# Relations 0 to 3 of a graph layer: seven half-size block products each in place of a full product, in two passes over the left operands, with sums of weight quarters on GpSimd

## The chip, the core and the metric

The kernel runs on one core of one Trainium2 chip. Its engines are TensorE (PE), VectorE (DVE), ScalarE (ACT), GpSimd (POOL) and SyncE (SP, which here only issues transfers). Each engine works through its own instructions strictly in the order in which the program lists them and waits for another engine or a transfer by a semaphore. The metric is the device time of one execution in microseconds (us).

## The reference, cut to what matters

The network takes x (1250 nodes, 1024 features) and 40000 edges (src, dst, type 0 to 7). The part that changes is the relational graph convolution:

```python
xn = _layernorm(x, axis=-1)
def _rgcn(x, edge_index, edge_type, weight, root, bias):
    out = x @ root + bias
    for r in range(8):
        mask = (edge_type == r)
        sums = segment_sum(x[src] * mask[:, None], dst)
        cnt = segment_sum(mask, dst)
        out = out + (sums / maximum(cnt, 1)[:, None]) @ weight[r]
    return out
```

A linear attention, two gates and an LSTM-like step follow, all with 1024x1024 weights and the same 1250 rows; the change doesn't touch them.

## The kernel before

**Products.** The kernel computes y_r = xn @ weight[r] for all eight relations first and gathers rows of y per edge afterwards. The work of TensorE is a list of stages. A stage is one half (512 columns) of one product; it has 10 units, one for each tile of 128 nodes. A unit is 24 matmuls of 512 columns into one PSUM bank: 8 blocks of the inner dimension, three matmuls each, since both operands are split into a high and a low part (`aThi`, `aTlo` for the left, `Whi`, `Wlo` for the weights). q numbers the units through the whole kernel, k the 8 blocks in a unit. The other engines' programs are written as a loop over the same (q, k), so that a step's place (q, k) sets its place in the order of its engine.

**Weights.** A stage's weights come in four granules of 128x1024 (512 KB). SP loads one into `Wraw`, ACT rounds it (`hi_w`, Whi), DVE subtracts (`lo_w`, Wlo). `Wraw` lies in the same bytes as `Wlo`. There are two sets, used by stages in turn, so the granules of stage s+1 are loaded, rounded and subtracted while stage s is computed.

**Results.** ACT copies a finished unit of y to one of three places of `res` (`evict`) and SP stores it to y_d (`store_unit`).

**Edges.** While relations 0 to 3 are computed, DVE also orders the edges: `count_below`, `run_codes`, `run_half`, `hold_half`, then for 2 halves x 10 tiles a `top_of` (five MAX8 with four MATCH_REPLACE8 between) and a `rank_tile`, and for each half `tables` and `tables_weights`. POOL reads 20 runs of codes (`read_run`, after `run_places` on DVE) and sends 10 rows of tables per half (`send_rows`, after `tables_weights`); SP then reads them back (`load_edges`, which waits for `sent[h]`). From q = 82 on POOL gathers rows of y (`gather`) and DVE adds them up (`add_edges`).

**The start.** x comes in ten tiles: LN on DVE (`ln_x`), TensorE turns the tile, ACT and DVE split it. POOL forms x + xn (`rows_sum`): tile 0, then the codes of the edges, then tiles 1 to 9. SP's `x_rows(t)` waits for `rows_sum(t)` and stores.

Of the kernel before, what the change touches and what calls it, by code (L numbers as in the profile page):

```python
# [5 lines left out]
F32 = mybir.dt.float32  # L6
# [74 lines left out]
Y_, R_, V_, K_, X_, G_, Q_, O_, C_, I_, T_, F_ = range(12)  # L81
STAGE = [(Y_, r, h) for r in range(R) for h in range(2)]
# [5 lines left out]
BY_ACT = (Y_, V_)  # L88
# [37 lines left out]
LN_AT = {1: 2, 2: 3, 4: 4, 6: 5, 7: 6, 8: 7, 9: 8, 10: 9}  # L126
TURN_AT = {1: 1, 3: 2, 5: 3, 7: 4, 8: 5, 9: 6, 10: 7, 11: 8, 12: 9}
# [90 lines left out]
def build(nc, x, src, dst, edge_type, weight, root, bias, w_gate, b_gate, Wq, Wk, Wv, Wg, bg, Wo,  # L218
          W_iT, b_i, W_oT, b_o, W_cT, b_c, out):
    with ExitStack() as ctx:  # L220
# [9 lines left out]
        xs_d = dram("xs_d", [N, D])  # L230
        y_d = [dram(f"y_d{h}", [HALF_R * N, D]) for h in range(2)]
# [110 lines left out]

        x_raw = at(M + 16448, "x_raw", [128, D], F32R)
# [27 lines left out]
        acc = ctx.enter_context(nc.psum_tensor("acc", [128, 3, H], F32))  # L371
        agg = ctx.enter_context(nc.psum_tensor("agg", [128, 2, H], F32))
# [3 lines left out]
        def turned_rows(w):  # L376
# [37 lines left out]
        v_in = [sem(f"v_in{i}") for i in range(2)]  # L414
        neg, expd, kv_zero, kv_done, kv_sb = (
            sem(n) for n in ("neg", "expd", "kv_zero", "kv_done", "kv_sb"))
        g_in = [sem(f"g_in{i}") for i in range(6)]
        num_done, num_out, gated, o_turned, o_hi, o_lo = (
            sem(n) for n in ("num_done", "num_out", "gated", "o_turned", "o_hi", "o_lo"))
        xs_in = [sem(f"xs_in{i}") for i in range(2)]  # L420
        tx_in = [sem(f"tx_in{i}") for i in range(2)]
        th_st = [sem(f"th_st{i}") for i in range(TH_SEMS)]
        u_in = [sem(f"u_in{i}") for i in range(U_SEMS)]
        th_tanh, th_made, u_turned, u_hi, u_lo = (
            sem(n) for n in ("th_tanh", "th_made", "u_turned", "u_hi", "u_lo"))
        c_in = [sem(f"c_in{i}") for i in range(3)]
        p_made, x1_made, x1_st, ln2_var, ln2_root, ln2_ready, ln2_done, x1_turned, x1_hi, x1_lo = (
            sem(n) for n in ("p_made", "x1_made", "x1_st", "ln2_var", "ln2_root", "ln2_ready", "ln2_done",
                             "x1_turned", "x1_hi", "x1_lo"))
        gate_act, cell, cell_th, out_made = (sem(n) for n in ("gate_act", "cell", "cell_th", "out_made"))  # L430
# [17 lines left out]
        def load_beside(q):  # L448

            if q < 20:  # L450
                return range(2 * GRAN, 3 * GRAN) if q == LAST[0] + 1 else range(0)
            s, i = UNIT[q]
            n = GRAN * (s + 1) + i
            return range(n, n + 1) if s + 1 < STAGES and i < GRAN else range(0)

        def split_beside(q):

            if q < 20:
                return {17: range(8, 9), 18: range(9, 11), 19: range(11, 12)}.get(q, range(0))
# [26 lines left out]
        def wait_evicted(engine, q):  # L486

            if KIND[q] in BY_ACT:
                engine.wait_ge(evac_a, BY_ACT_TO[q])
            else:  # L490
                engine.wait_ge(evac_v, BY_DVE_TO[q])

# [59 lines left out]
        def f_count(n):  # L552

            return 48 * len(range(n % 3, 2 * T, 3)) + 16 * (n // 3 + 1)
# [8 lines left out]
        def _(sp):  # L563
            def load_w(n):
                s, g = divmod(n, GRAN)
                if s >= 2:
                    sp.wait_ge(prod, LAST[s - 2] + 1)
                sp.dma_start(granule(Wraw, n), source_of(s)[g * 256:(g + 1) * 256, :].rearrange("(b p) n -> p b n", p=128)
                             ).then_inc(w_raw[n % (2 * GRAN)], 16)

            def load_x(t):
                sp.dma_start(xr[0:width(t), t % XS, :], x[rows(t), :]).then_inc(x_in[t % XS], 16)
# [11 lines left out]
            def load_bias(n):  # L584
                s = BIASED[n]
                if n >= 2:
                    wait_evicted(sp, LAST[BIASED[n - 2]])
# [102 lines left out]
            def load_o(t):  # L690
                g = min(t // 3, 2)
                if t == 3 * g:
                    sp.wait_ge(rows_st, 16 * (8 if g == 2 else 2 * g + 2))
                if t >= 2:
                    sp.wait_ge(o_in[t % 2], quarters_in(t - 2, 2))
# [97 lines left out]
            for n in range(4):  # L793
                load_w(n)
            load_x(1)
            load_w(4)
            load_w(5)
            load_x(2)
            load_w(6)
            load_w(7)  # L800
# [8 lines left out]
            def x_rows(t):  # L809

                sp.wait_ge(ln_done, with_halves(t))
                sp.dma_start(xn_d[rows(t), :], xnb[0:width(t), t % XS, :]).then_inc(xn_st[t % XS], 16)
                sp.wait_ge(xs_made, t + 1)
                sp.dma_start(xs_d[rows(t), :], xr[0:width(t), t % XS, :]).then_inc(xs_st[t % XS], 16)
# [7 lines left out]
            for q in range(UNITS + 1):  # L822
# [4 lines left out]
                if q < UNITS:  # L827
                    s, i = UNIT[q]
                    kind, _, h = STAGE[s]
# [1147 lines left out]
```

## Time and profile before

| | |
|---|---|
| median of three runs | 2173.67 us (2172.82 to 2173.79) |
| profiled execution, first to last instruction (span) | 2172.2 us |
| TensorE busy | 2156.8 us (99%) |
| VectorE busy | 1224.3 us (56%) |
| ScalarE busy | 441.0 us (20%) |
| GpSimd busy | 717.5 us (33%) |
| moved by DMA | 437.58 MB, mean 201 GB/s |

The span is the time from the first to the last instruction of one profiled execution; a run's device time is 1.5 us above it at the median. Busy time is an average over stages with different limits, so what a change of one stretch is worth has to be read in that stretch. A busy TensorE means that a matmul is in flight; the matmuls overlap.

### The profile page before, as it was taken

The numbers are of one execution on the slowest core, as the hardware profiler recorded it, in microseconds if no ns is written. First come the engines' busy times: TensorE is split into PE (matmuls) and PEld (weight loads), VectorE is DVE, ScalarE is ACT, GpSimd is POOL, SyncE is SP. The second block draws the span as 40 slices with busy tenths as digits, with TensorE's granted clock in tenths as the row PEclk, the third lists the DMA queues.
The fourth block names the chain that finished last, engine by engine and source line by source line (L and its number), as shares of the span: only waits on it lengthen the run. The fifth ranks groups of instructions, "written<-read, shape, count | busy, mean of one in ns | idle before, by whom it ended". The sixth has DMA issues, their size and how long they took to land.

```text
span 2172.2 us, 25195 instructions
## 1 busy us (share of the span) xinstructions
PE 2156.8 (99%) x9802; PEld 1744.3 (80%) x9802; DVE 1224.3 (56%) x1648; ACT 441.0 (20%) x618; POOL 717.5 (33%) x631
## 2 busy tenths in 40 slices
PE   8999999999999999999999999999999999999999
PEld 6877888888888888888878778889988888788877
DVE  6332678736666666676666567663355658534233
ACT  3221111211111111100221211112232313321121
POOL 4103002055555556553646445541221353000000
PEclk9999999999999999999999999999999999999999
DMA  6543321447688988793978888864169988604102
GB/s 255 191 133 94 111 87 48 132 165 240 233 296 288 306 307 287 248 307 94 339 238 291 282 272 297 304 206 159 68 184 265 295 288 260 176 16 132 56 28 80
DMA packets 217649, 437.58 MB, mean 201 GB/s; under 512 B 37381, under 2 KB 69812, under 8 KB 217530
## 3 DMA queue, kind: packets, MB, share of 16 engines
q1 hardware_dynamic: 146458, 239.60, 33.6%
q0 software_dynamic: 65248, 191.13, 26.7%
q10 hardware_dynamic: 5824, 5.25, 1.0%
q8 instruction: 77, 1.26, 0.2%
q14 instruction: 42, 0.34, 0.1%
HBM read 363.07 MB, written 113.90 MB: 220 GB/s over the span
## 4 chain that ended last, share of the span: by engine, by line
PE 98%; DVE 1%; ACT 0%; DMA 0%; issue 0%; SPq 0%; DVEq 0%; ACTq 0%
PE acc L1018 91%; PE acc L1013 5%; PE agg L951 1%; PE misc L936 1%; PE tp L900 0%; DVE Wlo L1211 0%; DMA x1n_d<-lnb 0%; DMA xr<-in_x 0%; PE agg L1026 0%; PE acc L1026 0%; DVE stats L1259 0%; DVE aTlo L1221 0%; ACT aThi L1045 0%; PE tp L908 0%; DVE res L1623 0%
## 5 line engine op out<-in xcount | busy, mean ns | idle before, releaser
L1018 PE MATMUL acc<-Whi,aThi 128*128 128x512 f32 (+1 forms) x2872 | 1136.2, 396 | 2.8 <-DVE A L1573 1.1
L1018 PE MATMUL acc<-Whi,aTlo 128*128 128x512 f32 (+1 forms) x2872 | 1131.9, 394 | 0.0
L1018 PE MATMUL acc<-Wlo,aThi 128*128 128x512 f32 (+1 forms) x2872 | 1128.5, 393 | 0.0
L1018 PEld LDWEIGHTS acc<-Whi,aThi 128*128 128x128 f32 (+1 forms) x2872 | 532.7, 185 | 134.5 <-DVE A L1573 1.5
L1018 PEld LDWEIGHTS acc<-Whi,aTlo 128*128 128x128 f32 (+1 forms) x2872 | 532.7, 185 | 133.5
L1018 PEld LDWEIGHTS acc<-Wlo,aThi 128*128 128x128 f32 (+1 forms) x2872 | 533.8, 186 | 131.9
L1818 POOL DMA_INDIRECT ring<-y_d,edge x390 | 482.4, 1237 | 430.0 <-DVE U L1443 156.9
L1211 DVE TENSOR_TENSOR Wlo<-Wraw,Whi 128x1024 fp32r<-128x1024 f32 x152 | 185.7, 1225 | 321.6 <-ACT Whi L1037 282.6
L1053 ACT COPY res<-acc 128x512 f32<-128x512 f32 (+1 forms) x180 | 105.7, 587 | 833.0 <-PE acc L1018 747.6
L1443 DVE SCALAR_TENSOR_TENSOR U<-ring,edge,U 128x1024 f32<-128x1024 f32 x180 | 230.3, 1279 | 16.6 <-DMA ring<-y_d,edge 16.3
L1443 DVE SCALAR_TENSOR_TENSOR odd<-ring,edge,odd 128x1024 f32<-128x1024 f32 x170 | 217.5, 1280 | 22.6 <-DMA ring<-y_d,edge 22.5
L1037 ACT CAST Whi<-Wraw 128x1024 fp32r<-128x1024 f32 x152 | 158.8, 1047 | 152.2 <-DMA Wraw<-in_L_mix_Wg 49.1
L1573 DVE TENSOR_TENSOR res<-acc,bias_sb 128x512 f32<-128x512 f32 x99 | 68.5, 692 | 214.0 <-PE acc L1018 126.7
L1805 POOL DMA_INDIRECT slot_d<-table,slot x20 | 21.7, 1087 | 227.9 <-DVEq L1403 222.4
L1114 ACT ACTIVATE res<-res 128x512 f32<-128x512 f32 (+1 forms) x59 | 37.4, 633 | 282.9 <-DVE res L1573 282.9
L1552 DVE SCALAR_TENSOR_TENSOR res<-acc,res 128x512 f32<-128x512 f32 (+3 forms) x44 | 28.0, 637 | 99.5 <-ACT res L1066 99.5
L1013 PE MATMUL acc<-aThi,Whi 128*128 128x384 f32 (+1 forms) x192 | 69.5, 362 | 0.0
L1940 POOL TENSOR_TENSOR og<-og,part 128x384 f32<-128x384 f32 (+1 forms) x32 | 27.7, 876 | 122.6 <-DVE part L1603 122.6
L1013 PE MATMUL acc<-aThi,Wlo 128*128 128x384 f32 (+1 forms) x192 | 67.6, 352 | 0.0
L1013 PE MATMUL acc<-aTlo,Whi 128*128 128x384 f32 (+1 forms) x192 | 67.5, 352 | 0.0
L1064 ACT ACTIVATE res<-acc 128x512 f32<-128x512 f32 (+3 forms) x44 | 24.4, 556 | 182.0 <-PE acc L1013 89.0
L1798 POOL DMA_INDIRECT runs<-code_d,run_row x20 | 21.1, 1054 | 100.4 <-DVEq L1299 94.7
(183 smaller groups left out, 1055.9 us busy)
## 6 DMA issues: line engine op xcount, KB each, us to landing
y_d<-res SPq DMA_DIRECT2D x144, 256.0 KB
Wraw<-in_L_gnn_weight SPq DMA_DIRECT2D x64, 512.0 KB
Wraw<-in_L_gnn_w_gate SPq DMA_DIRECT2D x16, 512.0 KB
ring<-y_d,edge POOLq DMA_INDIRECT x390
xr<-in_x SPq DMA_DIRECT2D x9, 512.0 KB, 4.7
xn_d<-xnb SPq DMA_DIRECT2D x9, 512.0 KB, 5.4
xs_d<-xr SPq DMA_DIRECT2D x9, 512.0 KB, 5.9
ur_d<-res SPq DMA_DIRECT2D x18, 256.0 KB
```

Of the source, the lines that this page charges most:

```text
L1013: mm = nc.tensor.matmul(to, a[:, s % 2, k, cols], b[:, k, c0:c0 + w], start=start, stop=stop)
L1018: mm = nc.tensor.matmul(to, a[:, k, rows(i)], b[:, s % 2, k, :], start=start, stop=stop)
L1037: nc.scalar.copy(granule(Whi, n), granule(Wraw, n)).then_inc(w_hi, 1)
L1053: nc.scalar.copy(res[0:width(i), q % 3, :], acc[0:width(i), q % 3, :]).then_inc(evac_a, 1)
L1064: nc.scalar.activation(a, p, ACT.Relu, scale=-1.0).then_inc(neg, 1)
L1114: nc.scalar.activation(a, a, ACT.Tanh if kind == T_ else ACT.Sigmoid).then_inc(gate_act, 1)
L1211: nc.vector.tensor_tensor(granule(Wlo, n), granule(Wraw, n), granule(Whi, n).bitcast(F32), ALU.subtract).then_inc(w_lo, 1)
L1443: nc.vector.scalar_tensor_tensor(to, g, scale, to, ALU.mult, ALU.add).then_inc(u_acc, 1)
L1552: nc.vector.scalar_tensor_tensor(a, p, 0.0, a, ALU.max, ALU.add).then_inc(evac_v, 1)
L1573: nc.vector.tensor_tensor(to, p, bias_sb[0:w, n % 2, :], ALU.add).then_inc(evac_v, 1)
L1818: pool.indirect_dma_start(ring[:, j % RING, :], None, a, bass.IndirectOffsetOnAxis(ap=index, axis=0), bounds_check=top - 1, oob_is_err=Fal ...
L1940: nc.gpsimd.tensor_tensor(o, o, part[0:w, a % 2, n, :], ALU.mult).then_inc(gated, 1)
```

## The change

Each y_r of relations 0 to 3 is now computed by blocks: the nodes are halved (2 x 625), and so are the inner dimension and the columns (512). Seven products of half size replace eight, with sums of quarters of the weights and of the left operand, and earlier results taken in again. Relations 4 to 7 and all later stages are as before.

- A block product has 5 units (m = 0 to 4, tiles of 125 nodes), and a unit now has 12 matmuls. Stages of four kinds come one kind after the other: AL (q 0 to 39), BE (40 to 79), GA (80 to 119), one stage for each relation, two products in each (p = 0 and 1); then DE (120 to 139), one product per relation. Where p = 1 follows in the same bank, it adds to what p = 0 left there, after that was copied out.
- Five banks are used in turn; `BEFORE[q]` is the unit whose copy must be done before unit q may start. In AL, BE and GA the order of units is m0 m1 of p = 0, m0 of p = 1, m2, m1, m3, m2, m4, m3, m4.
- Weights: BE needs eight loads of 512 KB and three sums of 128x1024 for each p on POOL (`add_quarters`), of which the third is stored to t4_d (`store_t4`) and read again for DE; GA needs six loads and one sum per p. BE's granules 2 and 3 are rounded only when the store of the third sum is done, since `Whraw` lies in the same bytes as `Whi`.
- All 140 units leave through a ring of four places (`made`); AL, BE and DE by ACT (`evict_made`), GA by DVE, which adds an earlier result (`evict_added`). The first product of BE and all of DE start from an earlier result that SP loads three units ahead (`load_part`) and ACT writes negated into the bank (`seed`).
- The left operand's four quadrants are combined on DVE (`make_right`), stored, and exchanged between the kinds of stages (six loads of 1.28 MB, `load_left`, split by `hi_left` and `lo_left`).
- The work on the edges is placed anew: `edge_at` puts old place (q, k) at 35 + (q - 17) x 13/8 new units.

```diff
+SEVEN = list(range(HALF_R))
+STAGE = [(AL_, r, 0) for r in SEVEN] + [(BE_, r, 0) for r in SEVEN] + [(GA_, r, 0) for r in SEVEN]
+STAGE += [(DE_, r, 0) for r in SEVEN[::2]]
+IN_TURN = [0, 1, 5, 2, 6, 3, 7, 4, 8, 9]
+UNIT = [(s, 5 * p + m) for m in range(3) for p in range(2) for s in range(2)]
+UNIT += [(s, 5 * p + m) for s in range(2) for p in range(2) for m in (3, 4)]
+UNIT += [(s, i) for s in range(2, STAGES) for i in
+         (range(10) if STAGE[s][0] == DE_ else IN_TURN if STAGE[s][0] in BLOCKED else range(units_of(s)))]
...
+        _at = [FIRST[_s] + d for d in {BE_: (5, 8, 9, 10), GA_: (4, 5, 6, 8)}.get(STAGE[_s + 1][0], (3, 5, 6, 8))]
...
+def edge_at(q, k):
+    return divmod(280 + (8 * (q - 17) + k) * 13 // 8, 8)
...
+            def store_made(q):
+                wait_evicted(sp, q)
+                sp.dma_start(block_rows(q), made[0:SIDE, q % OUT_RING, :]).then_inc(made_st[q % OUT_RING], 16)
...
+                    if q + 3 < BLOCK_UNITS and q + 3 in IN_PLACE:
+                        load_part(q + 3)
-                    if q == 76:
+                    if q == edge_at(76, 0)[0]:
                         load_edges(1)
...
+                if kind in BLOCKED:
+                    if BEFORE[q] is not None:
+                        wait_evicted(pe, BEFORE[q])
+                    if seeded_unit(q):
+                        pe.wait_ge(seeded, SEEDS_TO[q])
...
+                    for k in range(4):
+                        beside(q, k)
+                        if m == 0 and k % 2 == 0:
+                            pe.wait_ge(w_lo, SPLIT_RANK[GRAN * s + 2 * p + k // 2] + 1)
...
+            def evict_made(q):
+                if q >= OUT_RING:
+                    wait_made_stored(act, q - OUT_RING)
+                act.wait_ge(prod, q + 1)
+                nc.scalar.copy(made[0:SIDE, q % OUT_RING, :], acc[0:SIDE, BANK[q], :]).then_inc(evac_a, 1)
...
+            def evict_added(q):
+                n = IN_PLACE[q]
+                wait_made_stored(dve, q - OUT_RING)
+                dve.wait_ge(part_in[n % IN_RING], 16 * (n // IN_RING + 1))
+                dve.wait_ge(prod, q + 1)
+                nc.vector.tensor_tensor(made[0:SIDE, q % OUT_RING, :], acc[0:SIDE, BANK[q], :], in_place(q), ALU.add
+                                        ).then_inc(evac_v, 1)
...
+                add(second, granule(Whraw, n))
+                add(first, second)
+                add(granule(Whraw, n + 2), first)
...
+            for q in range(BLOCK_UNITS):
+                s = UNIT[q][0] + 1
+                if s > 2 and STAGE[s][0] in SUMS_IN:
+                    for p in range(2):
+                        if q == FIRST[s - 1] + 3 + 2 * p:
+                            add_quarters(s, p)
+                if q == edge_at(28, 2)[0]:
...
+                            read_run(i, t)
+                for h in range(2):
+                    if q == edge_at(59 + 15 * h, 1)[0]:
...
+                            send_rows(h, t)
```

Three places show what the new order puts side by side.

On DVE, before, these rows stood in the stage of relation 2 (`Wlo` is `lo_w`, MAX and MATCH_REPLACE are `top_of`, `above` and `rank` are `rank_tile`):

```order
L1211 TENSOR_TENSOR Wlo<-Wraw,Whi 128x1024
L1344 TENSOR_SCALAR above<-keyrow,key 128x1280
L1345 TENSOR_REDUCE rank<-above 128x1
L1355 MAX top_codes<-held 128x8
L1357 MATCH_REPLACE held<-top_codes,held 128x128
```

Now the same steps stand between the copies of GA's units (`made<-acc`); these are DVE's rows at q = 105 to 108:

```order
L1597 TENSOR_TENSOR Wlo<-Wraw,Whi 128x1024
L1640 TENSOR_TENSOR made<-acc,res 125x512
L1597 TENSOR_TENSOR Wlo<-Wraw,Whi 128x1024
L1640 TENSOR_TENSOR made<-acc,res 125x512
L1768 TENSOR_SCALAR above<-keyrow,key 128x1280
L1769 TENSOR_REDUCE rank<-above 128x1
L1640 TENSOR_TENSOR made<-acc,res 125x512
L1779 MAX top_codes<-held 128x8
```

What moved: rows that a bank, and with it TensorE, waits for now stand in this order, with steps of the edges between them.

On POOL, before, nothing stood between the last `rows_sum` and the sending of tables but the reads of runs:

```order
L1781 TENSOR_TENSOR xr<-xr,xnb 128x1024 [waits ln_done] x8
L1781 TENSOR_TENSOR xr<-xr,xnb 98x1024 [waits ln_done]
L1798 DMA runs<-code_d,run_row 128x64 [waits xn_st2,xs_st2,xs_st1,xn_st3,xn_st1,xs_st3,xs_st0,run_made,xn_st0,codes_st]
L1798 DMA runs<-code_d,run_row 128x64 x19
L1805 DMA slot_d<-table,slot 1280x82 [waits tabled,ranked]
```

Now at q = 53 to 55 (BE of relation 1; the sums are for BE of relation 2, which starts at q = 60):

```order
L2227 TENSOR_TENSOR Whraw<-Whraw,Wraw 128x1024 [waits w_sum_p_made]
L2260 DMA runs<-code_d,run_row 128x64 [waits xn_st2,xs_st2,xs_st1,xn_st3,xn_st1,xs_st3,xs_st0,run_made,xn_st0,codes_st]
L2260 DMA runs<-code_d,run_row 128x64 x19
L2227 TENSOR_TENSOR Wraw<-Wraw,Whraw 128x1024 [waits w_raw3,w_add_g_in1]
L2227 TENSOR_TENSOR Wraw<-Wraw 128x1024 [waits w_sum_p_made,w_raw1]
L2227 TENSOR_TENSOR Whraw<-Whraw,Wraw 128x1024 [waits w_sum_p_made]
```

What moved: the 20 reads stand between the sums for p = 0 and those for p = 1.

On SP, before, the second half's table was read at q = 76 in 11 transfers, the first of which waits for `sent[1]`. The last two of them and what stands behind:

```order
L668 DMA edge<-slot_d 128x24
L670 DMA whose<-slot_d 128x10x2
L620 DMA y_d<-res 128x512 [waits evac_a] x4
L620 DMA y_d<-res 98x512 [waits evac_a]
L568 DMA Wraw<-in_L_gnn_weight 128x2x512 [waits prod]
```

Now it is read at q = 130, again with the wait at the first of the 11; the earlier result for unit 133 is loaded ahead of them, that for unit 134 is the fifth row here:

```order
L941 DMA edge<-slot_d 128x24
L943 DMA whose<-slot_d 128x10x2
L840 DMA y_d<-made 125x512 [waits evac_a]
L760 DMA Wraw<-in_L_gnn_weight 128x2x512 [waits prod]
L835 DMA bias_sb<-y_d 125x512 [waits made_st_g_in1,seeded_ln2_root]
L840 DMA y_d<-made 125x512 [waits evac_a]
```

What moved: loads that TensorE needs within four units now queue behind the wait for `sent[1]`.

## Rows read from the trace of the kernel before

**Rows 1.** The page: busy time and share of the span, instructions
```profile
PE 2156.8 (99%) x9802; PEld 1744.3 (80%) x9802; DVE 1224.3 (56%) x1648; ACT 441.0 (20%) x618; POOL 717.5 (33%) x631
```

**Rows 2.** The chain that ended last: start us, us, what
```profile
89.76 372.25 PE acc L1018 x1608
```

**Rows 3.** Timeline of PE at its first matmuls: start us, us, engine
```profile
10.35 0.80 PE L1018 MATMUL acc<-Whi,aThi 128*128 128x512 f32 x1 [0.66 <-DVE aTlo L1668]
...
14.78 0.40 PE L1018 MATMUL acc<-Wlo,aThi 128*128 128x512 f32 x1
15.02 0.39 PE L1018 MATMUL acc<-Whi,aTlo 128*128 128x512 f32 x1
...
17.80 0.39 PE L1018 MATMUL acc<-Whi,aTlo 128*128 128x512 f32 x1
19.17 0.50 PE L1018 MATMUL acc<-Whi,aThi 128*128 128x512 f32 x1 [0.98 <-DVE Wlo L1211]
```

**Rows 4.** Busy time by stretch, with the columns of its heading
```profile
core 0: us, PE busy (x) PEld busy (x) DVE busy (x) ACT busy (x) POOL busy (x), PEclk, DMA share, GB/s
278.00:334.00 56.00, 56.00 (x243) 44.84 (x243) 41.39 (x109) 10.11 (x15) 0.00 (x0) 1.00 0.27 84
334.00:389.00 55.00, 55.00 (x240) 44.01 (x239) 42.11 (x107) 7.10 (x12) 11.23 (x10) 1.00 0.25 68
389.00:445.00 56.00, 56.00 (x244) 44.84 (x243) 43.94 (x98) 12.12 (x18) 5.27 (x5) 1.00 0.35 115
```

**Rows 5.** Timeline of DVE: one rank_tile, one top_of, the next rank_tile
```profile
313.48 0.88 DVE L1344 TENSOR_SCALAR above<-keyrow,key 128x1280 f32<-128x1280 f32 x1
...
315.92 0.29 DVE L1355 MAX8 top_codes<-held 128x8 f32<-128x128 f32 x1
...
319.12 0.89 DVE L1344 TENSOR_SCALAR above<-keyrow,key 128x1280 f32<-128x1280 f32 x1
```

**Rows 6.** Timeline of DVE: tables (to the Wlo) and tables_weights
```profile
341.36 0.17 DVE L1349 CAST slot<-rank 128x10 int32<-128x10 f32 x1
...
345.70 1.22 DVE L1211 TENSOR_TENSOR Wlo<-Wraw,Whi 128x1024 fp32r<-128x1024 f32 x1 [0.17 <-ACT Whi L1037]
...
352.49 2.03 DVE L1383 SCALAR_TENSOR_TENSOR of_r<-relation,weigh 128x400 f32<-128x400 f32 x4
...
361.29 0.89 DVE L1344 TENSOR_SCALAR above<-keyrow,key 128x1280 f32<-128x1280 f32 x1
```

**Rows 7.** Groups by line: busy us, mean ns, idle before and releaser
```profile
L1211 DVE TENSOR_TENSOR Wlo<-Wraw,Whi 128x1024 fp32r<-128x1024 f32 x152 | 185.7, 1225 | 321.6 <-ACT Whi L1037 282.6
L1573 DVE TENSOR_TENSOR res<-acc,bias_sb 128x512 f32<-128x512 f32 x99 | 68.5, 692 | 214.0 <-PE acc L1018 126.7
L1037 ACT CAST Whi<-Wraw 128x1024 fp32r<-128x1024 f32 x152 | 158.8, 1047 | 152.2 <-DMA Wraw<-in_L_mix_Wg 49.1
L1053 ACT COPY res<-acc 128x512 f32<-128x512 f32 (+1 forms) x180 | 105.7, 587 | 833.0 <-PE acc L1018 747.6
```

**Rows 8.** Groups of POOL by line, the same columns
```profile
L1781 POOL TENSOR_TENSOR xr<-xr,xnb 128x1024 f32<-128x1024 f32 (+1 forms) x10 | 23.9, 2401 | 46.2 <-DVE xnb L1274 25.1 <-DVE Wlo L1211 21.1
L1948 POOL TENSOR_TENSOR cring<-cring 128x512 f32<-128x512 f32 (+1 forms) x20 | 29.5, 1476 | 1.6
```

**Rows 9.** Timeline of POOL: the first and the last of the 20 reads of runs
```profile
175.02 1.28 POOL L1798 DMA_INDIRECT runs<-code_d,run_row  x1 [94.66 <-DVEq L1299]
...
200.88 1.00 POOL L1798 DMA_INDIRECT runs<-code_d,run_row  x1 [0.30 <-issue]
```

**Rows 10.** Timeline at 36 to 42 us: SP's queue, and ACT's copy
```profile
36.19 0.32 SPq L814 DMA_DIRECT2D xs_d<-xr  x1
...
37.03 0.78 SPq L620 DMA_DIRECT2D y_d<-res  x1
...
41.84 0.58 ACT L1053 COPY res<-acc 128x512 f32<-128x512 f32 x1 [7.08 <-DMA y_d<-res]
```

**Rows 11.** Timeline at 437 to 458 us: DVE, and SP's queue
```profile
437.27 0.17 DVE L1401 COPY table<-cnt 128x10 f32<-128x10 f32 x1
...
452.82 4.59 SPq L668 DMA_DIRECT2D edge<-slot_d  x10
457.46 0.44 SPq L670 DMA_DIRECT2D whose<-slot_d  x1
```

**Rows 12.** Transfers: issues with KB each, us to landing
```profile
xn_d<-xnb SPq DMA_DIRECT2D x9, 512.0 KB, 5.4
fx<-x_d SPq DMA_DIRECT2D x18, 256.0 KB, 3.7
```

**Rows 13.** SP's DMA queue at 302:357: packets, MB, share of 16 engines
```profile
q1 hardware_dynamic: 2427, 4.54, 26.6%
```

More of the change, by code:

```diff
@@ new lines @@
+for _q in range(UNITS):
+    if KIND[_q] not in BLOCKED:
+        _b = _q % 3
+    elif follows(_q):
+        _b = BANK[POS[UNIT[_q][0], UNIT[_q][1] - 5]]
+    else:
+        _b, _next = _next % 5, _next + 1
+    BANK.append(_b)
+    BEFORE.append(_holder.get(_b))
+    _holder[_b] = _q
+SEEDS_TO = [sum(KIND[p] in BLOCKED and seeded_unit(p) for p in range(q + 1)) for q in range(BLOCK_UNITS)]
+SEEDS = SEEDS_TO[-1]
+IN_UNITS = [q for q in range(BLOCK_UNITS) if seeded_unit(q) or KIND[q] == GA_]
+IN_PLACE = {q: n for n, q in enumerate(IN_UNITS)}
@@ new lines, with unit_of, relation_of, made_by @@
+IN_RING = 5
+OUT_RING = 4
+def unit_of(kind, r, p, m):
+    return POS[STAGE.index((kind, r, 0)), 5 * p + m]
+def relation_of(q):
+    r = STAGE[UNIT[q][0]][1]
+    return r + half_of(q)[0] if KIND[q] == DE_ else r
+def made_by(q):
+    r, (p, m) = relation_of(q), half_of(q)
+    if KIND[q] == BE_:
+        return unit_of(AL_, r, 0, m)
+    return unit_of(BE_, r, 1 - p if KIND[q] == GA_ else 1, m)
+def quadrant(q):
+    p = half_of(q)[0]
+    return {AL_: (0, 1 - p), BE_: (p, 1 - p), GA_: (1 - p, 1), DE_: (1, 0)}[KIND[q]]
@@ L340, in build @@
         assert M + 41024 + up(16 * COLS) + 32 * T <= end and RING * 4096 == 20480
+        made = at(M + 45312, "made", [128, OUT_RING, H])
+        assert M + 45312 + 2048 * OUT_RING <= end
         x_raw = at(M + 16448, "x_raw", [128, D], F32R)
@@ L567, in load_w, with fetch, quarter @@
                     sp.wait_ge(prod, LAST[s - 2] + 1)
-                sp.dma_start(granule(Wraw, n), source_of(s)[g * 256:(g + 1) * 256, :].rearrange("(b p) n -> p b n", p=128)
-                             ).then_inc(w_raw[n % (2 * GRAN)], 16)
+                kind, r, _ = STAGE[s]
+                def fetch(a, n, of, done):
+                    sp.dma_start(granule(a, n), of.rearrange("(b p) n -> p b n", p=128)).then_inc(done, 16)
+                def quarter(up_down, side_half, p):
+                    first = up_down * H + p * 256
+                    return weight[r][first:first + 256, half(side_half)]
@@ L1154, in _ @@
                 half_k = slice(4 * h, 4 * h + 4)
-                nc.scalar.copy(aThi[:, half_k, rows(0)], turned_rows(128)[:, half_k, :]).then_inc(x_hi, 1)
-            for n in range(2, 5):
+                nc.scalar.copy(aThi[:, half_k, side(0)], turned_rows(SIDE)[:, half_k, :]).then_inc(x_hi, 1)
+            for n in SPLIT_ORDER[2:5]:
                 hi_w(n)
+            keep_x(0)
             root_x(1)
-            for n in range(5, 8):
+            for n in SPLIT_ORDER[5:8]:
                 hi_w(n)
```

532 lines of the change are left out of this document (404 added, 128 removed).

## Prediction

> **What bounds the kernel now.** First the busy shares: TensorE is in work for 99% of the span [rows 1]. Then the chain that ended last, which from 89.76 us on is 1608 matmuls in one piece [rows 2]: 231.5 ns a matmul, 5.56 us a unit of 24. No other engine holds TensorE up in the stretch that changes. Third, busy time by stretch, since an average hides what is near its limit: between 278 and 445 us VectorE works 127.4 of 167 us [rows 4], 76%, and TensorE doesn't notice, because nothing in VectorE's queue but `lo_w` is needed by TensorE there. The reader should keep both facts: a gain on TensorE counts in full as long as nobody else is late, and VectorE has only a quarter of its time left where the edges are ordered.
>
> **What is removed.** 8 half products of 10 units x 24 matmuls become 14 stages of 10 units x 12: 1920 matmuls become 1680. A stage of the change has 27.8 us of matmuls (10 x 12 x 231.5 ns), a unit 2.78 us. 240 x 231.5 ns = 55.6 us less. This is the whole gain. The turning of x by TensorE stays.
>
> **What is added at the start.** `made` has four places, and unit 5 is copied out only when unit 1 is stored. Unit 7 adds to unit 5's bank, so it waits for that copy. SP's row for unit 1's store stands behind `x_rows(1)`, which waits for POOL: before, that store of x issued at 36.19 us and the first store of y at 37.03, and ACT's copy that waited for it came at 41.84 [rows 10]. Before, TensorE had units of 5.56 us to cover this. Now unit 7 would start at 34.9 us (24 matmuls end at 18.2, the next start at 19.2, behind a `lo_w`, as now [rows 3], then five units of 2.78 and some 2 for turning two tiles); it can start at 42: +7 us. Two smaller waits of the kind (weights for stage 2, loaded and awaited by ACT within one unit; `keep_x` ahead of the turning of tile 4) I put at 2. Term: +9, from 4 (the store lands sooner) to 14.
>
> **What is added in BE (q 40 to 79).** A sum of quarters costs what POOL's add of 128x1024 costs, 2.4 us [rows 8]; three for each p, 14.4 of 27.8 us: hidden. One place isn't. In the stage that starts at q = 50, POOL's order is the sums for p = 0, the 20 reads of runs, the sums for p = 1. The reads wait for `run_places` on DVE at q = 53, behind `lo_left` at q = 52, which needs ACT after unit 51: about 12.5 us after q = 50 starts. The 20 reads take 26.9 us [rows 9] (175.02 to 201.9), to 39.4. Three sums, to 46.6; `lo_w`, 1.2 [rows 7]: 47.8. Unit 60 needs this granule after half its matmuls, at 29.2. The third sum is then stored (512 KB, 5.4 us to landing [rows 12]) before `hi_w` (1.05) and, behind it on ACT, the copy of unit 60 (0.59) [rows 7]: unit 62 starts at 54.0 where 33.4 was due. Term: +21; from 14, if the reads start early, to 28. Otherwise the store of a third sum lands at 31.7 and unit 52, 62, 72 wait for a copy at 33.4: due in the same moment, 0.
>
> **What is added in GA (q 80 to 119).** Here VectorE copies out the units, and its queue also holds the edges. From the copy of unit 80 to that of unit 119 the order lists: 40 copies at 0.69 (the row of `res<-acc,bias_sb` has the same shape [rows 7]) = 27.6; 16 `lo_w` at 1.2 = 19.2; 4 `lo_left` of 1250 columns at 1.5 = 6.0; 16 `rank_tile` at 2.44 and 16 `top_of` at 3.20 [rows 5] = 39.0 and 51.2; one `tables` and one `tables_weights`, 4.3 and 8.8 [rows 6] = 13.1. Sum 156 us, for 39 units of 108.4 us of matmuls. VectorE is over its time by 44%. It can't fall behind instead: unit p = 1, m0 stands two places behind p = 0, m0 and needs its copy. So TensorE goes at VectorE's pace. Working: VectorE enters 4.3 us late (`top_of`, `rank_tile`, `top_of` behind the last `lo_w` of BE); the work from unit 80's copy to unit 117's, the last that unit 119 needs, is 156 less 12 = 144; idle meanwhile 2.2 (unit 82 isn't done) and 5.7, since `lo_w` at q = 105 waits for a sum that stands behind POOL's ten sends (taken at 1.28 each, as one read of [rows 9]: 12.8 us); then unit 119, 2.8. 4.3 + 144 + 7.9 + 2.8 = 159, against 108.4: +50. From 40, if a bank in hand saves a unit per stage, to 56.
>
> **What is added in DE (q 120 to 139).** VectorE is still behind: it needs 25.8 us from the start of q = 120 to reach `tables_weights` of the second half, which ends at 34.6. Before, from the end of that step (437.4) to SP's being free again (457.9) it took 20.5 us [rows 11]: ten sends, the landing, eleven transfers. So SP is free at 55.1. Then come a store, a granule, and the earlier result for unit 134, 256 KB in 3.7 us and more [rows 12], and the seed: 61.4. Unit 134 was due at 14 x 2.78 = 38.9. Before, SP stood here as long and nobody missed it. Term: +22, from 12 to 27.
>
> **Transfers.** BE's first stage moves 11.6 MB (8 granules, two left quadrants, third sums, 10 stores, 5 results), the later ones 9.1, GA's first 10.8. In a mix of loads and stores 26.6% of 55 us moved 4.54 MB [rows 13]: 310 GB/s if the engines were full. At that rate 11.6 MB take 37.5 us, 10 over the stage; 9.1 take 29.3. The lateness falls before unit 60's wait, which swallows it, and GA's first stage lasts 36 us anyway. Term +1, from 0 to 10.
>
> **The clock.** The first ten matmuls start 0.43 us apart (10.35 to 14.78), then 0.23 [rows 3]: the levels of 1.2 and 2.4 GHz, 2.0 us lost. The trace of before has no long idle time of TensorE, so it can't show whether four waits of 7 to 20 us bring the low level back: 0 to 8 us; I take 4, in the middle, because the nearest row is a start from rest. The Trainium skill (TensorE: Matmul & The Clock Gate, Part 1) says that an idle array falls back to 1.2 GHz and that activity releases it; by that rule each of the four pays its 2.0, and the sum is 4 higher.
>
> **A rule against the change.** An add on POOL of 128x512 takes 1476 ns [rows 8] where half of 2401 would be 1200, with VectorE at work beside it. The Trainium skill (SBUF — State Buffer, SBUF: two separate sides) calls the port pair of the two an exclusive lock when VectorE reads two operands in SBUF. Worked from the rows, as a mechanism of this kernel: 32 sums x 2.4 = 77 us of POOL, 19 of them in GA, where 25 of VectorE's 156 us have two such operands, so 3 us more there.
>
> **Sum.** -55.6 + 9 + 21 + 50 + 22 + 1 + 4 = +51. The profiled execution's span is 2172.2; the median is 1.5 above it. 2173.7 + 51 = 2225; I say 2224.
>
> **Rivals.**
> - All covers hold. TensorE alone decides as it does now; 2173.7 - 55.6 + 9 = 2127, faster. For it: VectorE at 76% never held TensorE up. Against it: a copy of GA then was not in that queue. It decides from the point where VectorE's work in GA is under 111 us; it counts 156. The place is one, the copies in GA; the other two waits would have to be hidden too. A part of it (steps of the edges overlap the matmuls better than I count) gives 2135 to 2165. Together 0.10.
> - VectorE bounds GA, but POOL's reads and SP's wait are both hidden: 2173.7 - 55.6 + 9 + 50 = 2177 to 2183. 0.09, half of it in the band of no change.
> - One of those two is hidden: 2203. 0.19.
> - All as summed: 2212 to 2240. 0.52.
> - Everything summed, and the DMA engines or the shared port add 10 to 20 more: 2240 to 2260. 0.10.
>
> **Range and chances.** The likeliest is the fourth. 2190 to 2245 holds it, most of the third and part of the last, some 8 in 10. A measurement of this kernel tells from no change what is over 0.2%, 4.3 us. Faster than 2169.4: 0.10; within: 0.04; slower: 0.86.
>
> **What would show it.** In the profile after: PE has 240 fewer matmuls; VectorE in GA busy for 95% and more, the stretch q 80 to 119 lasting about 159 us, and TensorE's waits there charged to `made<-acc`; a PE wait near 18 us at `Wlo` with POOL's reads just before; one near 20 us ahead of unit 134, with SP idle for `slot_d`. From the second kind of Y stages on (relations 4 to 7) all as before. Wrong it would be if GA's units ran at 2.8 us each: then VectorE's steps in that stretch are shorter than their rows, or TensorE has more banks in hand than I see.

## The result and the profile after

The changed kernel took 2526.6 us (2520.17 to 2531.75, four runs) against 2173.6: a ratio of 1.162 (95% interval 1.160 to 1.165), slower. The direction was forecast; the size, +353 us where +50 was forecast, lies far outside the range.

The page of the changed kernel, busy time and share (as [rows 1]), then its 40 slices:

```profile
PE 2196.0 (87%) x9562; PEld 1752.3 (69%) x9562; DVE 1311.7 (52%) x1725; ACT 520.3 (21%) x731; POOL 798.7 (32%) x663
...
PE   5626665775665999999999999999999999999999
...
PEclk8867887887878999999999999999999999999999
DMA  4435664554453868888784978788534899832212
```

PE has 240 matmuls fewer, as forecast, and is short of work in the first 13 slices, all of relations 0 to 3; after that it is as full as before. In the same slices the granted clock (PEclk) is at 6 to 8 tenths.

Busy time of the changed kernel by kind of stage, AL, BE, GA, DE (columns as in [rows 4]; the cuts are the starts of units 0, 40, 80, 120 and of relation 4):

```profile
15.00:287.00 272.00, 148.91 (x553) 114.41 (x554) 75.66 (x113) 58.08 (x93) 48.34 (x43) 0.77 0.46 160
287.00:492.00 205.00, 137.29 (x479) 103.75 (x479) 66.44 (x89) 54.20 (x81) 68.56 (x40) 0.82 0.58 190
492.00:706.00 214.00, 136.48 (x484) 103.11 (x483) 156.21 (x358) 22.97 (x23) 25.36 (x16) 0.81 0.49 168
706.00:821.00 115.00, 69.66 (x243) 50.66 (x243) 33.98 (x54) 33.58 (x50) 15.49 (x11) 0.82 0.45 152
```

All four are long, AL by most, where hardly anything was forecast. VectorE works 156 of 214 us in GA: the forecast counted 156 us of work and took it for the bound, but the stretch is 55 us longer still. PE's waits in the changed kernel (waited for, us, times, longest):

```profile
PE acc L1308 <- ACT made L1408: 145.3, 19, 55.6
PE acc L1308 <- ACT acc L1401: 87.5, 25, 18.7
PE acc L1308 <- DVE made L1640: 73.0, 15, 12.7
```

The reader should not stop at ACT. Its copies wait for places of `made` and for weights, which SP's transfers bring. Transfers of the changed kernel from 100 to 175 us, in 40 slices, with the queue's total:

```profile
DMA  3333333699963333332333333223349339775001
GB/s 113 117 117 125 122 96 107 252 318 360 389 259 123 118 114 117 116 113 100 127 132 126 113 122 120 94 75 92 99 128 285 115 133 289 208 238 194 25 25 58
...
q1 hardware_dynamic: 4275, 11.19, 43.1%
```

This is the line that tells the case. The busy share stands at 3 tenths in 23 of the 40 slices, mostly at 100 to 130 GB/s, and leaves this level upward only for short pieces of 2 to 4 times the rate. With too little to do the share would come and go down to 0, as it does in the kernel before in its later stages. A level held at about 5/16 looks like five engines working without a pause and eleven idle. The trace's packets, counted one by one, agree: from 100 to 115 us exactly five are in flight for about 80% of the time, over the whole of AL (15 to 287 us) for 55%; 16 and more are for 14% of AL. In GA (492 to 706 us) the level shows again, as the value that the slices keep coming back to (two lie below it):

```profile
DMA  3397755335735675533334776454343355553333
GB/s 128 131 282 257 243 194 191 127 128 167 230 127 191 199 248 193 195 127 127 126 127 137 242 239 200 154 179 143 133 69 81 127 191 198 195 194 127 127 127 127
```

127 GB/s are 25.4 GB/s for each of five engines. SP's queue and ACT at the longest wait, the 55.6 us ahead of unit 18:

```profile
140.63 8.15 SPq L1087 DMA_DIRECT2D xs_d<-xr  x1
148.83 1.92 SPq L843 DMA_DIRECT2D xr<-in_x  x1
150.79 3.64 SPq L840 DMA_DIRECT2D y_d<-made  x1
154.48 10.71 SPq L760 DMA_DIRECT2D Wraw<-in_L_gnn_weight  x4
```
```profile
171.73 1.04 ACT L1363 CAST Whi<-Wraw 128x1024 fp32r<-128x1024 f32 x1 [46.67 <-DMA Wraw<-in_L_gnn_weight]
172.68 0.58 ACT L1408 COPY made<-acc 125x512 f32<-125x512 f32 x1
```

SP itself stands 2 to 8 us at the issue of one transfer (before the 8.15 it waits for nothing: the sum that this store sends was made at 128 us). The weights for stage 2 are issued behind rows of x and results and land at 171; ACT's rounding waits for them, and the copy that TensorE needs stands behind it.

The Trainium skill (DMA: Bandwidth & Descriptors, section on why a DMA increments its semaphore by 16 and not by 1) says how many engines a transfer gets: the largest number up to 16 that divides the slowest dimension of both sides. It gives 10 for 100 partitions; for 125 that makes 5. By this rule 125 rows keep 5/16, 0.31, of the engines busy, and the trace's level is 0.33; the runs below test it. The prediction didn't use the rule, and it speaks directly against this change, which went from tiles of 128 rows to 125.

### The profile page after: what moved, and what is told of

It is laid out like the page before. It is cut to its first block, busy times and chain, and to the rows that moved or that the text cites. A ratio compares the mean times of both kernels' runs of the same rounds, so it can differ in the third digit from the quotient of the medians.

```text
span 2529.7 us, 25469 instructions
## 1 busy us (share of the span) xinstructions
PE 2196.0 (87%) x9562; PEld 1752.3 (69%) x9562; DVE 1311.7 (52%) x1725; ACT 520.3 (21%) x731; POOL 798.7 (32%) x663
## 4 chain that ended last, share of the span: by engine, by line
PE 67%; DMA 2%; SPq 1%; issue 0%; POOL 0%; DVE 0%; ACT 0%; ACTq 0%; DVEq 0%
PE acc L1337 61%; PE acc L1332 4%; PE acc L1243 1%; DMA bias_sb<-y_d 1%; PE misc L1228 0%; DMA res<-y_d 0%; DMA zx<-x1n_d 0%; PE acc L1345 0%; POOL slot_d L2267 0%; SPq L941 0%; SPq L840 0%; SPq L760 0%; PE acc L1308 0%; DMA slot_d<-table,slot 0%; PE misc L1243 0%
## 5 line engine op out<-in xcount | busy, mean ns | idle before, releaser
L1337 PE MATMUL acc<-Whi,aThi 128*128 128x512 f32 (+1 forms) x2232 | 882.7, 395 | 2.0 <-DVE A L1997 2.0
L1337 PE MATMUL acc<-Whi,aTlo 128*128 128x512 f32 (+1 forms) x2232 | 879.6, 394 | 0.0
L1337 PE MATMUL acc<-Wlo,aThi 128*128 128x512 f32 (+1 forms) x2232 | 877.2, 393 | 0.0
L1308 PE MATMUL acc<-Whi,aThi 128*125 128x512 f32 x560 | 260.5, 465 | 313.1 <-ACT made L1408 145.3
L1337 PEld LDWEIGHTS acc<-Wlo,aThi 128*128 128x128 f32 (+1 forms) x2232 | 414.8, 186 | 102.6
L1308 PEld LDWEIGHTS acc<-Whi,aThi 128*125 128x125 f32 x560 | 122.4, 218 | 370.2 <-ACT made L1408 153.8
L1308 PE MATMUL acc<-Wlo,aThi 128*125 128x512 f32 x560 | 250.3, 447 | 0.0
L1308 PE MATMUL acc<-Whi,aTlo 128*125 128x512 f32 x560 | 247.6, 442 | 0.0
L1308 PEld LDWEIGHTS acc<-Whi,aTlo 128*125 128x125 f32 x560 | 122.3, 218 | 33.0
L1308 PEld LDWEIGHTS acc<-Wlo,aThi 128*125 128x125 f32 x560 | 123.1, 220 | 28.1
## 6 DMA issues: line engine op xcount, KB each, us to landing
Wraw<-in_L_gnn_weight SPq DMA_DIRECT2D x80, 512.0 KB, 11.6
```

The lines of the kernel that those rows point to most:

```text
L1308: mm = nc.tensor.matmul(to, a[:, a_k, own], b[:, s % 2, b_k, :], start=start, stop=stop, skip_group_check=True)
L1337: mm = nc.tensor.matmul(to, a[:, k, rows(i)], b[:, s % 2, k, :], start=start, stop=stop)
```

## The experiments

**Is it the five engines?** The changed kernel with every transfer of 125 rows issued in two parts, and the waits on its semaphores doubled:

```diff
+            def in_parts(to, of, done):
+                for c in (slice(0, 112), slice(112, SIDE)):
+                    sp.dma_start(to[c], of[c]).then_inc(done, 16)
-                sp.dma_start(block_rows(q), made[0:SIDE, q % OUT_RING, :]).then_inc(made_st[q % OUT_RING], 16)
+                in_parts(block_rows(q), made[0:SIDE, q % OUT_RING, :], made_st[q % OUT_RING])
...
-            engine.wait_ge(made_st[q % OUT_RING], 16 * (q // OUT_RING + 1))
+            engine.wait_ge(made_st[q % OUT_RING], 32 * (q // OUT_RING + 1))
```

> The changed kernel, with each transfer of 125 rows (x in, xn_d, xs_d, results out, earlier results in) issued as two, of 112 and of 13 rows. Theory A (a transfer of 125 rows runs on only 5 of the 16 DMA engines, and these 5 hold the stretch of relations 0 to 3 up; the DMA share stands at 0.33 and about 127 GB/s over much of it): all 16 are used now, the plateau goes, and what is left is what the prediction summed: 2225 us, 2190 to 2260. Theory B (SP's single queue and the number of transfers hold it up, whatever engines move them): twice as many issues, 2530 to 2600. Theory C (DVE, POOL and SP waits alone, larger than predicted): no change, 2500 to 2540.

Measured 2321.0 us (2317.5 to 2324.1). 206 us came back for the price of twice as many issues: B and C fall. It is still 60 us above A's upper end.

> As the run before, but cut into 115 and 10 rows: the same number of issues and nearly the same sizes, 115 = 5 x 23 and 10 = 10 x 1, so that the busiest engine carries 24 rows of each where it carried 25 (and 8 in the cut of 112 and 13). Theory A: the time stays near the changed kernel's, 2490 to 2530. Theory B, or any in which two transfers in place of one help or harm by themselves: the same time as the cut of 112 and 13.

Measured 2502.2 (2499.8 to 2504.1). The same two issues, but 115 and 10 rows: 24 us come back for 206. So it isn't the splitting. Two more cuts fill the scale:

> The changed kernel with each transfer of 125 rows cut into 95 and 30: 95 = 5 x 19 and 30 = 15 x 2, so that the busiest engine carries 21 rows of each. The uncut kernel (25 rows, 2527 us) and the cut of 115 and 10 (24 rows, 2502) lie 24 us apart for one row; from the bytes, 70.6 MB in such transfers are 0.56 MB a row, at 25.4 GB/s 22 us. Theory A: 2527 - 4 x 24 = 2430, 2410 to 2450. If two smaller transfers in place of one are what helped, it lies near the cut of 115 and 10, 2490 to 2510.

Measured 2453.6, just above its range.

> The same with 100 and 25 rows: 10 x 10 and 5 x 5, 15 rows on the busiest engine. Theory A: the slope of 24 us a row would give 2287, below the 2321 of 8 rows, where the busiest engine no longer decides; so it lies at that floor or a little over it, 2320 to 2360. If something else than the busiest engine's rows sets the time: 2400 or more.

Measured 2372.1, 12 above A's range and well under the 2400 of the other reading. In order of the rows on the busiest engine, 25, 24, 21, 15 and 8: 2526.6, 2502.2, 2453.6, 2372.1, 2321.0. It falls at every step, by 24, 16, 14 and 7 us a row. A was right in the order of the five times and in the size of the first step alone. It expected 22 to 24 us a row all the way down to a floor; over the 17 rows it is 12 on average. The likely reason, which no run isolates, is that other waits decide more and more places as the busiest engine gets less to do.

> Only the transfers of x (in, xn_d, xs_d; 27 transfers of 500 KB between 15 and 287 us) cut into 112 and 13 rows. Theory A: the busiest engine carries 1.9 MB less by then, at 25.4 GB/s 74 us: about 2450, all of it won before q = 40. Theory B or C: 2520 to 2540.

Measured 2456.5: -70 us for -74 worked out. AL fell from 271.6 to 201.1; BE (205.6 to 206.8) and GA (213.3 to 212.4) stayed.

> Only the transfers of results (out and in again) cut into 112 and 13 rows. Theory A: 56 us less in AL, and in BE, GA and DE down to what the prediction summed for them (about -73, -54, -37): about 2305, 2270 to 2350. Theory B: 2530 to 2590. Theory C: no change.

Measured 2383.8, 34 above A's range: AL came back by 43 where 56 was worked out, BE, GA and DE by 38, 42 and 22, for 73, 54 and 37. C falls here too.

The reverse, on the kernel before:

```diff
+                if in_two(q):
+                    sp.dma_start(to[0:125], of[0:125]).then_inc(res_st[q % 3], 16)
+                    to, of = to[125:128], of[125:128]
                 sp.dma_start(to, of).then_inc(res_st[q % 3], 16)
```

> The kernel before, with each of its 72 stores of a full tile of y (128 rows) in relations 0 to 3 cut into 125 rows and 3. By theory A the engines that take the 125 rows carry 26 rows for 8, 2.6 MB more on the busiest engine over 444 us, 104 us of its time at 25.4 GB/s; their share goes from about 30% to 55%. The theory says that such a transfer costs nothing while the 5 engines have room: no change, 2170 to 2178. If a transfer of 125 rows cost by itself (its own landing, which ACT's copy waits for), 2190 and more.

Measured 2177.8 (2177.0 to 2179.4) beside 2174.0, a ratio of 1.0019 (1.0009 to 1.0029): inside the range, though not quite nothing. So a transfer of 125 rows is nearly free in a stretch whose DMA share is 38% on average.

**The waits that the prediction named, in the cut kernel.** With the five engines out of the way they can be read one by one. Here are, all in the cut kernel (every transfer of 125 rows in parts of 112 and 13), POOL from the sums for p = 0 to those for p = 1 (the first and the last read of 20), ACT with a rounding, a copy and a seed, and TensorE at unit 60:

```profile
232.30 2.59 POOL L2231 TENSOR_TENSOR Wraw<-Wraw,Whraw 128x1024 f32<-128x1024 f32 x1 [15.56 <-DMA Whraw<-in_L_gnn_weight]
...
237.53 2.41 POOL L2231 TENSOR_TENSOR Whraw<-Whraw,Wraw 128x1024 f32<-128x1024 f32 x1
240.12 2.30 POOL L2264 DMA_INDIRECT runs<-code_d,run_row  x1 [0.18 <-issue]
...
266.19 1.00 POOL L2264 DMA_INDIRECT runs<-code_d,run_row  x1 [0.31 <-issue]
267.21 2.35 POOL L2231 TENSOR_TENSOR Wraw<-Wraw,Whraw 128x1024 f32<-128x1024 f32 x1
```
```profile
272.13 1.04 ACT L1367 CAST Whi<-Wraw 128x1024 fp32r<-128x1024 f32 x1 [26.60 <-POOL Wraw L2231]
273.08 0.58 ACT L1412 COPY made<-acc 125x512 f32<-125x512 f32 x1
273.56 0.60 ACT L1405 ACTIVATE acc<-res 125x512 f32<-125x512 f32 x1
```
```profile
274.26 0.76 PE L1312 MATMUL acc<-Whi,aThi 128*125 128x512 f32 x1 [23.82 <-ACT made L1412]
```

The change that moves the reads:

```diff
-                if q == edge_at(28, 2)[0]:
+                if q == 56:
```

> All transfers of 125 rows cut into 112 and 13 (2321 us), and the 20 reads of runs on POOL moved from q = 53 to q = 56, behind the quarter sums for p = 1 of the stage at q = 60. Theory A (what the prediction said of BE: the wait of 23.8 us ahead of unit 60 comes from the reads that stand between the sums): that wait goes, with the 2 us at the low clock behind it: 2295, 2285 to 2302. Rival (the DMA engines, busy in BE, deliver the weights of that stage as late anyway): the wait stays at 15 us or more, 2310 to 2325.

Measured 2305.4 (2304.5 to 2308.1), 15.5 less, between the two. The wait ahead of unit 60 is gone, but the reads now stand ahead of the sums for the stage at q = 70. POOL and TensorE in this kernel:

```profile
276.29 1.00 POOL L2264 DMA_INDIRECT runs<-code_d,run_row  x1 [0.30 <-issue]
277.31 2.35 POOL L2231 TENSOR_TENSOR Wraw<-Wraw,Whraw 128x1024 f32<-128x1024 f32 x1
```
```profile
284.39 0.76 PE L1312 MATMUL acc<-Whi,aThi 128*125 128x512 f32 x1 [8.14 <-ACT acc L1405]
```

Unit 67 waits 8.1 us for a seed that stands behind ACT's rounding of that sum; in the cut kernel it waited 1.7. The stall moved with the reads and lost two thirds of its size. SP's queue in the cut kernel, around its wait for `sent[1]`, and TensorE at unit 134:

```profile
558.98 0.76 SPq L826 DMA_DIRECT2D bias_sb<-y_d  x2
580.05 4.61 SPq L945 DMA_DIRECT2D edge<-slot_d  x10
584.71 0.43 SPq L947 DMA_DIRECT2D whose<-slot_d  x1
585.19 1.07 SPq L826 DMA_DIRECT2D y_d<-made  x2
586.31 0.40 SPq L760 DMA_DIRECT2D Wraw<-in_L_gnn_weight  x1
586.80 0.89 SPq L826 DMA_DIRECT2D bias_sb<-y_d  x2
```
```profile
594.28 0.76 PE L1312 MATMUL acc<-Whi,aThi 128*125 128x512 f32 x1 [23.55 <-ACT acc L1405]
```

The change that moves SP's wait:

```diff
-                    if q == edge_at(76, 0)[0]:
+                    if q == 138:
                         load_edges(1)
```

> The cut of 112 and 13 (2321 us), and SP's load_edges(1), with the wait for sent[1], moved from q = 130 to q = 138, behind the last load_part; the check of the edges that needs it on DVE and PE moved from q = 135 to 137 to q = 140 and 141. Theory A (the wait of 23.6 us ahead of unit 134 is SP's, for POOL's sends): it goes, 2295, 2288 to 2305. Rival (the wait moves to the made ring, since store_made(137) and the stores behind it now stand behind sent[1], or to the check of the edges at q = 141): 2305 to 2325.

Measured 2291.6 (2287.7 to 2297.3), 29 less, inside A's range. DE fell from 94.1 to 68.1 us, and the wait ahead of unit 134 is gone.

> The cut of 112 and 13 (2321 us), with the steps on the edges spread anew: denser in BE, 14 of the 35 old places of ordering in GA (2.8 new units for an old one, where it was 1.6), the rest in DE and the first units of relation 4; the reads of runs in two parts of ten, at q = 47 and 56; load_edges(1) at q = 139; the sums over edges on DVE begin at q = 148 in place of 142. So it also takes both waits of the two runs before away. Theory A (VectorE's queue bounds GA; 57.8 us over the matmuls there): GA falls from 169 us to 125 or less, and the time to 2321 - 26 - 26 - 45 = 2224, 2205 to 2245. Rival (GA is held up by transfers as AL is): GA stays above 145 us, 2245 to 2280.

The edit is a table of places in place of one slope, with the other moves as the expectation lists them:

```diff
+EDGE_KNOTS = ((17, 35), (28.25, 47.5), (36.25, 61), (41, 66), (50, 80), (64, 119), (76, 139), (80, 144))
```

Measured 2255.2 (2247.1 to 2259.9), 66 less, 10 above A's range and inside the rival's (2245 to 2280, GA above 145). The profile is of the fastest of its runs, 2247.1. Busy time by kind of stage, the cut kernel first, then this one:

```profile
12.00:181.00 169.00, 130.10 (x553) 102.61 (x554) 81.70 (x113) 59.64 (x94) 48.45 (x43) 0.89 0.84 266
181.00:350.00 169.00, 123.80 (x479) 95.41 (x480) 85.70 (x98) 53.09 (x78) 73.76 (x40) 0.86 0.74 234
350.00:520.00 170.00, 129.53 (x486) 99.48 (x485) 148.96 (x334) 22.74 (x23) 25.72 (x16) 0.87 0.68 207
520.00:614.00 94.00, 61.42 (x244) 47.91 (x243) 40.38 (x70) 32.94 (x50) 14.66 (x11) 0.82 0.58 183
```
```profile
12.00:176.00 164.00, 130.30 (x552) 102.64 (x550) 79.88 (x112) 59.08 (x94) 48.84 (x43) 0.90 0.84 270
176.00:328.00 152.00, 124.99 (x482) 97.08 (x483) 98.39 (x148) 53.48 (x79) 75.76 (x40) 0.87 0.81 265
328.00:473.00 145.00, 119.09 (x479) 92.74 (x478) 119.93 (x240) 22.19 (x22) 27.56 (x16) 0.92 0.76 239
473.00:535.00 62.00, 57.43 (x244) 44.63 (x243) 52.73 (x106) 33.43 (x51) 0.86 (x1) 1.00 0.83 270
```

With 29 us of VectorE's work taken out of GA, GA is 23 us shorter (145.6 for 169.0): its queue bounded a good part of GA. DE, at a granted clock of 1.00, is within 6 us of its matmuls. But GA at 145.6 us is not at the 125 forecast, and VectorE is busy for 83% of it: this run alone doesn't exclude that transfers hold the rest of GA, as the rival says. The new places also cost something behind the stretch: what follows takes 1710.5 us for 1704.6, with a wait of 3.5 us in relation 4's first stage that the cut kernel doesn't have.

**What holds the rest?** DMA is at 76 to 84% in the last table, so capacity was the next suspect.

> The kernel with all transfers of 125 rows cut and the edges spread anew (2255 us), which leaves out 112 of the 125 rows of every earlier result that is read in again from the sixth on (what lies in those rows is older data), 17 MB of the 136 MB that the stretch moves, all in BE, GA and DE; the number of transfers stays. Theory D (with all 16 DMA engines in use, their capacity, 80% busy over the stretch, is now what is left of the loss): 17 MB at 300 GB/s are 57 us of transfer time, of which the part in BE and GA that isn't under VectorE's or POOL's waits comes back: 2225, 2205 to 2240. Rival (chains of waits between engines, not the amount moved): 2248 to 2258.

Measured 2245.8 (2242.6 to 2246.5), between the two ranges. That is 9 under the median of the kernel that it starts from, but that kernel scatters over 13 us, and against its fastest run, the profiled one, it is 1 us. By the two traces GA takes 141.1 for 145.6, DE 56.0 for 61.3 (its matmuls are 55.6) and BE 152.6 for 151.5, while AL, which the edit doesn't touch, takes 3.4 more and what follows the stretch 4.5 more. So the amount moved accounts for at most some 10 of the 124 us left, none of it in BE: the rival, nearly. D falls as the main cause in BE and GA. The edit leaves every transfer in its place, so it says nothing of what their number costs.

> The same kernel (2255 us), complete, with the four granules for stage 2 issued by SP at the head of its work for q = 16, ahead of the rows of x and the stores of results that stood before them (issued at 89.0 us, landed at 96.0, wanted at 79 in the cut kernel). If the 16.5 us wait ahead of unit 18 is only this place in SP's queue: it shrinks to 8 or less, 2246. If it is the DMA engines' capacity in AL (94% busy between 60 and 100 us): the others get later in turn, 2252 to 2258.

Measured 2247.9 (2247.0 to 2248.9). The wait ahead of unit 18 went from 16.5 to 10.8 us, AL from 164.7 to 163.0. Even this is hard to tell from scatter: in the other traces whose program is the same up to there the wait is 12.7, 13.2, 14.4 and 17.3 us. The 7 us of difference in the medians lie within the scatter of the kernel that it starts from (2247 to 2260). So the times don't tell the two readings apart; that the wait didn't shrink to 8 speaks against the first. Leaving transfers of x out of AL wasn't tried.

## Why the prediction was wrong

Loss by kind of stage over TensorE's own time (from before, less 55.6 us: 132.9 us to the end of AL, then 111.2, 111.2 and 55.6), worked from the starts of units 0, 40, 80 and 120 and the end of 139. The forecast's 107 is its own sum of +51 before the 55.6 are taken off; what follows the stretch takes 1704.6 to 1710.5 us, 1706.0 before. All are from the profiled executions.

```
        forecast   changed   cut 112+13   and edges spread anew
AL        9         153.8       47.9        43.2
BE       22          94.4       58.5        40.4
GA       50         102.1       57.8        34.4
DE       22          59.9       38.5         5.9
clock     4         (in the four above)
sum     107         410         203         124
```

- **What is removed**: right. 1680 matmuls; a unit without a wait lasts 2.8 us.
- **Transfers, "+1, from 0 to 10"**: the step that failed, and the reason for the miss. It took 310 GB/s from [rows 13], a window with tiles of 128 rows, and used it for transfers of 125 rows; and it began to count at BE, though AL has the most. 70.6 of the 136 MB of the stretch go in transfers of 125 rows. Each of the five engines then carries a fifth of those and a sixteenth of the rest: 24.3 / 5 + 19.1 / 16 = 6.05 MB in AL, at 25.4 GB/s 238 of its 272 us; for BE 180 of 206, GA 203 of 213, DE 94 of 115 in the same way. That is nearly the whole of each (an estimate: the trace doesn't name a packet's engine). The cut to 112 and 13 rows took 206 us off, where the term was 1. The rest of the miss stays in the cut kernel, 203 us of loss for 107: 39 over the forecast in AL, 36 in BE, 8 in GA, 16 in DE. The next points are about these.
- **The start, +9**: far too small even with all engines in use: AL loses 47.9 in the cut kernel. Unit 7, the place that it names, waits 2.0 us there; unit 2, which it doesn't, waits 8.5, for copies that stand on ACT behind roundings of weights that land late. The largest part is the wait ahead of unit 18, put at 2 with the like and found at 14.4 us there: weights of stage 2 stand behind rows of x in SP's queue while the DMA engines are busy. From 60 to 100 us of the cut kernel:

```profile
q1 hardware_dynamic: 5259, 12.71, 94.5%
```

- **BE, +21**: the cause and the size held at its place, the path didn't. Unit 60 of the cut kernel waits 23.8 us, and by the run that moves them the 20 reads make the wait. But they begin 21.9 us after unit 50 (which starts at 218.2) and not 12.5, since the sums for p = 0 wait for weights until 232.3; and unit 60 waits at its first matmul, for a copy and a seed that stand on ACT behind a rounding (272.13 to 274.16), not for `lo_w` after half its matmuls. That the size came out near is in part luck. BE loses 58.5 in all; the waits of 1 to 5 us, for `lo_left`, seeds and `lo_w`, and the low clock behind them weren't forecast.
- **GA, +50**: 57.8 in the cut kernel, and moving 29 us of VectorE's work out made GA 23 shorter. The mechanism held for that part; of the 34 us left, fewer bytes took 4.5 and the rest is open. "Busy for 95% and more" was wrong, VectorE is at 88% (73% in the changed kernel): between its own pieces it waits too.
- **DE, +22**: unit 134 waits 23.6 us in the cut kernel, 18.7 in the changed one, and the move of one wait on SP's queue took 29 off. Right at its place; DE loses 38.5 in all, with 7.4 us ahead of unit 124 that weren't forecast.
- **The clock, +4**: mis-sized. A wait costs up to the 2 us said, but the forecast counted four. In the changed kernel about 330 matmuls of the stretch start 0.43 us apart (the level of 1.2 GHz) where 0.23 is the full rate, some 65 us together; in the cut kernel about 170, 33 us; after the edges are spread about 115, 22 us. These are within the losses of the table and are not independent of their waits: where VectorE or a transfer decides, a faster matmul would only wait longer.
- **The rule against the change** (one port pair for VectorE and POOL, 3 us more in GA): about the right size in GA. Each VectorE step that lies beside a POOL sum, less the median of the same step with none beside it (over these kernels and the one before), gives in GA 1.9 us together in the changed kernel, 5.2 in the cut one and 5.7 with the edges spread. The count in the prediction took only steps with two operands in SBUF, but `above`, which reads one and a value for each row, is longer too; and it took GA alone, where BE of the cut kernel has some 18 us of the kind. In the kernel with the edges spread, steps of VectorE, the POOL sums that lie beside them, and one VectorE step with a sum beside it (409.02) and without (431.56):

```profile
276.24 3.56 DVE L1752 SCALAR_TENSOR_TENSOR within<-runs,within 128x1280 f32<-128x1280 f32 x1
```
```profile
275.67 2.79 POOL L2237 TENSOR_TENSOR Wraw<-Wraw 128x1024 f32<-128x1024 f32 x1
278.54 3.53 POOL L2237 TENSOR_TENSOR Whraw<-Whraw,Wraw 128x1024 f32<-128x1024 f32 x1
...
408.70 2.39 POOL L2237 TENSOR_TENSOR Wraw<-Wraw,Whraw 128x1024 f32<-128x1024 f32 x1 [27.84 <-DMA Whraw<-in_L_gnn_weight]
```
```profile
409.02 2.75 DVE L1778 TENSOR_SCALAR above<-keyrow,key 128x1280 f32<-128x1280 f32 x1
...
431.56 0.88 DVE L1778 TENSOR_SCALAR above<-keyrow,key 128x1280 f32<-128x1280 f32 x1
```

POOL's sum takes 3.5 where it takes 2.35 alone, VectorE's `within` 3.56 where it takes 1.49 in the kernel before, and its `above` 2.75 where it takes 0.88. What of this reaches TensorE no run isolates.

None of the rivals was near. All but the last combined waits between engines; the last gave the DMA engines or the shared port 10 to 20 us. None asked how fast a transfer of the new shape is.

**What stays open.** Best measured of the versions with the change is 2248 us (with 2255 the same within its scatter), 3.4% above the kernel before. The 124 us that are left with the edges spread lie 43 in AL, 40 in BE, 34 in GA and 6 in DE. The stretch (15 to 821 us) moves 136 MB where the kernel before moved 56 (10 to 466 us), by the transfer views of the changed kernel and of the kernel before:

```profile
DMA packets 70223, 135.78 MB, mean 168 GB/s; under 512 B 9493, under 2 KB 10118, under 8 KB 70195
```
```profile
DMA packets 32267, 56.47 MB, mean 124 GB/s; under 512 B 8907, under 2 KB 9532, under 8 KB 32242
```

With the edges spread, waits of 7 to 17 us stand ahead of units 18, 45, 70 and 108, for a copy on ACT, a seed, a `lo_w` and a copy on VectorE. Which of these is worth what wasn't taken further.

## What to carry to other kernels

Before a tile's height is changed, look at every transfer of that tile: here transfers of 125 rows kept about five packets in flight, those cut into 112 and 13 rows up to sixteen, and that cut gave back 206 of 353 us. The DMA share that stood still at 5/16 was the sign; the mean over AL, 46%, hid it. And where a scheme saves matmuls by earlier results and sums, count its bytes first: this one saved 12.5% of the stretch's matmuls and moved 2.4 times the data, and TensorE had no wait in the stretch to give away.

## What the runs showed of the hardware that was not expected

- Transfers of 125 rows ran at 127 GB/s in all, with five packets in flight, 25.4 GB/s for each. Transfers of 128 rows behind them in the same queue came late too: the loads of weights landed 11.6 us after their issue (median over the whole kernel), 7.6 in the cut kernel. Four cuts of the same bytes gave times in the order of the rows on the busiest engine.
- SP stood at the issue itself: 8.15 us for one transfer in the changed kernel, 0.4 for one in the rows of the cut kernel.
- Splitting costs little: twice the issues of 250 KB transfers left DE within 6 us of its matmuls.
- Many waits of a few us cost clock as well, which the prediction left open. In the changed kernel the ten matmuls behind the wait of 16.85 us ahead of unit 60 start 0.43 us apart (1.2 GHz), and so do those behind 4.15 us ahead of unit 55; six of the ten behind 2.12 us ahead of unit 137 do. Behind 1.97 us ahead of unit 123 and behind 2.39 us ahead of unit 136 all start 0.23 us apart (2.4 GHz).
